# Attention and routed-expert layer on one core: the row maxima reach the score operand through TensorE and ScalarE instead of a transfer, with a new order of the work

## What is computed

```python
q, k, v = x @ wq + bq, x @ wk + bk, x @ wv + bv      # 16 heads of 8; rotary turn of q and k
scores = einsum('bhqd,bhkd->bhqk', q, k) / sqrt(8) + causal
x = layernorm(x + (softmax(scores) @ v) @ wo + bo)
idx = argmax(softmax(x.reshape(4096, 128) @ wg))     # 8 experts, first 512 tokens of each kept
x = layernorm(x + gate * (x @ W[idx].T + b[idx]))    # zero for tokens beyond an expert's 512
```

## Time and profile before

| | |
|---|---|
| median of 3 runs | 418.27 us (418.15 to 418.33) |
| the profiled execution | 417.29 us, span 415.5 us |
| busy in the span | TensorE 340.7, VectorE 326.3, ScalarE 269.9, GpSimd 285.5 us |
| DMA | 48.76 MB, 150727 packets; hardware queue of SyncE 58.9% of 16 engines' span, of ScalarE 3.0% |

### The profile page before, as it was taken

One profiled execution on the slowest core, in us unless ns is written; L12 is line 12 of the kernel. 1 busy time (PEld: TensorE's weight loads), 2 busy tenths in 40 slices (PEclk: granted clock), 3 DMA queues, 4 the chain that ended last, 5 costly groups with the idle time before them and its releaser, 6 DMA issues.

```text
span 415.5 us, 11631 instructions
## 1 busy us (share of the span) xinstructions
PE 340.7 (82%) x4230; PEld 279.9 (67%) x4230; DVE 326.3 (79%) x871; ACT 269.9 (65%) x633; POOL 285.5 (69%) x508
## 2 busy tenths in 40 slices
PE   4445596989989988898899989998999896987781
PEld 4334384868777877787777868786878785866561
DVE  5678664768989997999898989998989985875454
ACT  5252385758677866868595859695968585778500
POOL 6273337376688877787778787888879785575543
PEclk9968587999999999999999999999999999999976
DMA  5297948686968586857767676768586869310000
GB/s 153 76 174 143 144 114 127 106 147 117 143 120 160 108 141 132 163 100 148 138 134 132 138 136 126 146 118 167 110 162 113 157 112 165 24 43 2 16 13 25
DMA packets 150727, 48.76 MB, mean 117 GB/s; under 512 B 113311, under 2 KB 146979, under 8 KB 150670
## 3 DMA queue, kind: packets, MB, share of 16 engines
q1 hardware_dynamic: 144766, 43.70, 58.9%
q10 hardware_dynamic: 5184, 2.36, 3.0%
q0 software_dynamic: 720, 1.97, 1.5%
HBM read 28.60 MB, written 14.68 MB: 104 GB/s over the span
## 4 chain that ended last, share of the span: by engine, by line
PE 39%; DVE 14%; DMA 13%; ACT 13%; SPq 8%; issue 7%; POOL 2%; ACTq 2%; DVEq 0%; POOLq 0%
DMA q_plain<-max_rows 7%; DMA q_diag<-plain_parts 6%; PE ps_m L1051 4%; PE ps_ab L1137 4%; PE ps_ab L1121 4%; PE ps_pv L1152 4%; ACT high L693 3%; PE ps_m L1053 3%; PE ps_m L1052 3%; PE ps_ab L1105 3%; ACT ps_ab L697 3%; SPq L445 3%; SPq L489 3%; DVE row_max L911 2%; DVE low L901 2%
## 5 line engine op out<-in xcount | busy, mean ns | idle before, releaser
L693 ACT ACTIVATE high<-ps_ab 128x448 f16<-128x448 f32 (+1 forms) x192 | 100.9, 525 | 41.6 <-PE ps_ab L1121 40.9
L911 DVE TENSOR_REDUCE row_max<-ps_ab 128x2 f32<-128x512 f32 (+3 forms) x176 | 109.5, 628 | 12.7 <-PE ps_ab L1137 12.4
L540 POOL TENSOR_TENSOR low<-probs,high 128x384 f16<-128x384 f32 (+1 forms) x64 | 64.4, 1016 | 13.0 <-ACT probs L697 11.7
L901 DVE TENSOR_TENSOR low<-ps_ab,high 128x448 f16<-128x448 f32 (+1 forms) x80 | 47.1, 589 | 28.3 <-ACT ps_ab L697 28.3
L697 ACT ACTIVATE ps_ab<-ps_ab 128x448 f32<-128x448 f32 (+1 forms) x128 | 67.7, 529 | 0.0
L1121 PE MATMUL ps_ab<-q_plain,k_diag 128*128 128x128 bf16 (+1 forms) x768 | 66.5, 214 | 0.0
L1137 PE MATMUL ps_ab<-k_plain,q_diag 128*128 128x192 bf16 (+3 forms) x512 | 66.1, 243 | 0.0
L1152 PE MATMUL ps_pv<-v_mov,high 128*128 128x64 bf16 x768 | 64.6, 194 | 0.9 <-ACT low L701 0.7
L1152 PE MATMUL ps_pv<-v_mov,low 128*128 128x64 bf16 x768 | 64.4, 193 | 0.0
L1099 PE MATMUL ps_ab<-mask_a_bf,ident_bf 128*128 128x128 bf16 (+2 forms) x176 | 45.3, 257 | 19.5 <-DMA q_diag<-plain_parts 12.6
L1105 PE MATMUL ps_ab<-mask_b_bf,ident_bf 128*128 128x128 bf16 (+1 forms) x192 | 47.5, 247 | 15.2 <-DMA q_plain<-max_rows 6.1
(11 more groups left out here) (188 smaller groups left out, 928.5 us busy)
## 6 DMA issues: line engine op xcount, KB each, us to landing
plain_parts<-rot SPq DMA_DIRECT2D x180, 64.0 KB, 2.2
k_plain<-plain_parts SPq DMA_DIRECT2D x16, 384.0 KB, 4.2
q_diag<-plain_parts SPq DMA_DIRECT2D x32, 192.0 KB, 5.6
q_plain<-plain_parts SPq DMA_DIRECT2D x16, 384.0 KB, 4.8
k_diag<-plain_parts SPq DMA_DIRECT2D x32, 192.0 KB, 4.2
v_mov<-v_parts SPq DMA_DIRECT2D x64, 48.0 KB, 2.0
x_in<-in_L_attn_x_dram SPq DMA_DIRECT2D x16, 128.0 KB, 5.4
out_dram<-y_out POOLq DMA_DIRECT2D x15, 128.0 KB, 2.5
```

Source lines behind the costliest of these rows:

```text
L540: pool.tensor_tensor(fine(low, k), kept_probs(k), fine(high, k), ALU.subtract).then_inc(s_["low_pool"], 1)
L693: act.activation(fine(high, k), b_scores(k), ACT.Exp, scale=SCALE)
L901: dve.tensor_tensor(fine(low, k), b_scores(k), fine(high, k), ALU.subtract)\
L911: last = dve.tensor_reduce(row_max[:, NBLK - 1 - j, groups[0]:groups[-1] + 1], scores[:, :, col:col + width(j)], AX.X, ALU.max)
```

## The change

- `max_parts` gets 96 zero columns at its front, then 24 columns for each row block and half of the heads. "ex" becomes eight matmuls of 64 columns, whose stationary operand is a window of 120 columns that ends with the 24 wanted, so that the parts come out in rows 96 to 119 of `ps_n`, 256 columns for each half of the heads.
- ScalarE copies rows 96 to 119 of `ps_n` straight into `q_plain`, 24 rows of 4 x 256 columns, twice. `max_rows`, its two DMAs and the semaphore of their landing go. The copies wait for `b_ready` of two sequences earlier, b0 for `maxrows_done`.
- `LOWS` goes from DPADPDADPDAP to DPADPDDPDDAP: chunk 6 goes from way A to D and chunks 8 and 9 swap P and D for D and D with chunk 7 now P. Six rests lie on VectorE (chunks 0, 3, 5, 6, 8, 9), four on GpSimd (1, 4, 7, 11), two on ScalarE (2, 10).
- SyncE's list in a step becomes: x_in; the six writes of rot_1; q_plain; first half of k_diag; the four writes of rot_2; the two of rot_3; second half of k_diag; k_plain and q_diag once the writes have landed; v_mov.
- All positions are new. Around the maxima TensorE's order becomes: loc, b11, pv7, pv8, pv9, sub10, **ex**, e0, e1, pv10, pv11, a0, **b0**, b1, a1, e2, a2, e3, a3, turn, b2, a4, b3, y. ScalarE keeps exp of b11, low10, **maxrows**, rot1, copy, exp of b0. VectorE: a10, last logits piece, low9, the last gate piece of the sequence before, kept, rope, add, inv, gate, statistics, gate, sel0, gate, inv, a0, a1, low0. GpSimd: low4, out, low7, parts, seen, low11, rot, norm, rest pieces, low1.

The diff, less the tables of positions that are not spoken of:

```diff
-LOWS = "DPADPDADPDAP"
+LOWS = "DPADPDDPDDAP"
 PE_AT = dict(
-    b=(162, 163, 167, 169, 177, 180, 183, 190, 197, 198, 203, 208),
+    b=(176, 178, 187, 189, 195, 198, 205, 211, 215, 217, 222, 227),
-    a=(91, 93, 97, 100, 104, 114, 118, 123, 124, 127, 132),
-    pv=(171, 186, 189, 192, 199, 206, 207, 213, 215, 216, 218, 220), ex=147, turn=230, y=234, x1t=249, logits=259,
-    loc=268, v=112, xt=1, qk=9, e=(274, 278, 288, 293))
+    a=(111, 115, 118, 120, 124, 132, 133, 137, 145, 150, 154),
+    pv=(199, 207, 210, 213, 220, 221, 225, 228, 230, 231, 236, 238), ex=169, turn=250, y=254, x1t=270, logits=276,
+    loc=290, v=129, xt=2, qk=27, e=(298, 299, 309, 311))
...
-        max_parts = sb("max_parts", [128, NBLK, 64], bf)
-        max_rows = sb("max_rows", [2 * MAX_ROWS, S], bf)
+        max_parts = sb("max_parts", [128, SCORE_ROWS + NBLK * 2 * MAX_ROWS], bf)
...
                     after(sp, "y_ready", n - KEPT + 1)
                     sp.dma_start(x_in[n % KEPT][:, :, :], of_seq(x_t, n)).then_inc(s_["x_loaded"], 16)
-                if b_ahead:
-                    after(sp, "b_ready", b - 2, NB, NB)
-                    load_q_plain(b, p)
...
                 if b_ahead:
+                    after(sp, "b_ready", b - 2, NB, NB)
+                    load_q_plain(b, p)
                     load_k_diag(b, p, 0)
                 write(rot_2, 1, "rot2_done")
+                write(rot_3, 2, "rot3_done")
                 if b_ahead:
                     load_k_diag(b, p, 1)
-                write(rot_3, 2, "rot3_done")
-                if has(b) and not is_step(s, 0):
-                    load_v(b, p)
                 if has(a):
                     after(sp, "parts_written", a, PARTS_WRITTEN, PARTS_WRITTEN)
...
-                if is_step(s, 0):
+                if has(b):
                     load_v(b, p)
...
                         after(act, "ex_ready", b, 1, 1)
-                        after(act, "maxrows_loaded", b, 2 * 16)
-                        for jj in range(2):
-                            last = act.activation(max_rows[:, :].rearrange("m (i jj r) -> m jj i r", i=2, jj=2)[:, jj],
-                                                  ps_n[64 * jj:64 * jj + 2 * MAX_ROWS, 0:2 * BLK]
-                                                  .rearrange("m (i r) -> m i r", i=2), ACT.Copy)
+                        after(act, "b_ready", b - 2, NB, NB)
+                        for half_at in range(2):
+                            last = act.activation(q_plain[pb_][SCORE_ROWS:ONE_ROW, 4 * half_at:4 * half_at + 4, :],
+                                                  ps_n[SCORE_ROWS:ONE_ROW, S * half_at:S * half_at + S].unsqueeze(1)
+                                                  .broadcast_to([MAX_ROWS, 4, S]), ACT.Copy)
                         last.then_inc(s_["maxrows_done"], 1)
-                        after(act, "maxrows_done", b, 1, 1)
-                        after(act, "pv_ready", b - 2, NB, NB)
-                        for half_at in range(2):
-                            act.dma_start(q_plain[pb_][SCORE_ROWS:SCORE_ROWS + MAX_ROWS, 4 * half_at:4 * half_at + 4, :],
-                                          max_rows[MAX_ROWS * half_at:MAX_ROWS * half_at + MAX_ROWS, :].unsqueeze(1)
-                                          .broadcast_to([MAX_ROWS, 4, S])).then_inc(s_["maxrows_loaded"], 16)
...
-                            after(pe, "maxrows_loaded", c, 2 * 16, 2 * 16)
+                            after(pe, "maxrows_done", c, 1, 1)
...
-                        for i in range(NBLK // 2):
-                            mm = pe.matmul(ps_n[:, BLK * i:BLK * i + BLK],
-                                           max_parts[:, 2 * i:2 * i + 2, :].rearrange("p i m -> p (i m)"), stacked_bf[:, :],
-                                           start=(i == 0), stop=True, skip_group_check=True)
+                        for half_at in range(2):
+                            for j in range(NBLK):
+                                at, to = MAX_ROWS * (2 * j + half_at), S * half_at + BLK * j
+                                mm = pe.matmul(ps_n[0:ONE_ROW, to:to + BLK], max_parts[:, at:at + ONE_ROW], stacked_bf[:, :],
+                                               start=(half_at == 0 and j == 0), stop=True, skip_group_check=True)
```

More of the change, by code:

```diff
@@ L64 @@
 N_FIRST = 4
-LOWS = "DPADPDADPDAP"
+LOWS = "DPADPDDPDDAP"
 SLOTS = 64
 PE_AT = dict(
-    b=(162, 163, 167, 169, 177, 180, 183, 190, 197, 198, 203, 208),
-    sub=(153, 172, 174, 175, 181, 184, 194, 200, 202, 205, 209, 212),
-    a=(91, 93, 97, 100, 104, 114, 118, 123, 124, 127, 132),
-    pv=(171, 186, 189, 192, 199, 206, 207, 213, 215, 216, 218, 220), ex=147, turn=230, y=234, x1t=249, logits=259,
-    loc=268, v=112, xt=1, qk=9, e=(274, 278, 288, 293))
+    b=(176, 178, 187, 189, 195, 198, 205, 211, 215, 217, 222, 227),
+    sub=(180, 191, 192, 202, 204, 208, 216, 223, 224, 229, 232, 237),
+    a=(111, 115, 118, 120, 124, 132, 133, 137, 145, 150, 154),
+    pv=(199, 207, 210, 213, 220, 221, 225, 228, 230, 231, 236, 238), ex=169, turn=250, y=254, x1t=270, logits=276,
+    loc=290, v=129, xt=2, qk=27, e=(298, 299, 309, 311))
@@ L74 @@
 ACT_AT = dict(
-    b=(151, 152, 154, 157, 192, 193, 194, 196, 202, 204, 205, 209),
-    low=(155, 156, 158, 159, 160, 198, 199, 200, 206, 207, 210, 212), copy=(201, 214), attn=217, x1h=259, xh=5,
-    v1=97, maxrows=147, rot1=21, egate=267, route=272)
+    b=(152, 153, 157, 158, 192, 193, 198, 199, 203, 205, 208, 210),
+    low=(155, 156, 159, 160, 196, 197, 200, 201, 204, 206, 211, 214), copy=(202, 215), attn=218, x1h=259, xh=2,
+    v1=97, maxrows=148, rot1=21, egate=271, route=273)
 DVE_AT = dict(
-    low=(160, 163, 165, 167, 172, 174, 177, 193, 195, 205, 206, 221),
@@ L80 @@
-    a=(89, 91, 94, 97, 100, 105, 109, 111, 128, 134, 140), sel=(280, 290), inv=(212, 218), add=339, z1=230,
-    x1=(234, 235), stats2=341, x1l=240, xl=5, vrest=104, lg=(258, 260, 263, 264, 265, 266), rope=16,
-    g=(271, 274, 278, 279, 284))
+    low=(163, 169, 171, 172, 192, 193, 197, 203, 205, 209, 213, 225),
+    a=(96, 98, 101, 103, 104, 110, 113, 130, 134, 137, 143), sel=(285, 294), inv=(217, 223), add=344, z1=234,
+    x1=(239, 240), stats2=347, x1l=259, xl=4, vrest=109, lg=(263, 264, 266, 268, 270, 272), rope=22,
@@ L83 @@
+    g=(276, 282, 284, 286, 338))
 POOL_AT = dict(
-    low=(129, 135, 136, 139, 141, 143, 145, 146, 148, 149, 150, 192), norm=(195, 196), rs1=202, parts=80, vparts=76,
-    seen=211, rot=2, rest=(5, 6, 9), out=334)
-LAST_AT = [dict(e=(286, 287, 301, 307), sel=(287, 331), add=337), dict()]
+    low=(128, 134, 136, 137, 140, 142, 143, 144, 147, 148, 149, 150), norm=(194, 195), rs1=202, parts=81, vparts=75,
+    seen=210, rot=1, rest=(4, 5, 7), out=333)
+LAST_AT = [dict(e=(305, 313, 328, 331), sel=(292, 339), add=343), dict(g=(276, 282, 284, 286, 319))]
@@ L262, in layer_kernel @@
         names += """w_loaded vw_loaded ident_loaded late_loaded tables_loaded x_loaded parts_written
-                    aops_loaded0 aops_loaded1 bops_loaded0 bops_loaded1 maxrows_loaded v_loaded
+                    aops_loaded0 aops_loaded1 bops_loaded0 bops_loaded1  v_loaded
                     one_loaded stored""".split()
@@ L320, in max_part @@
         def max_part(i):
-            return max_parts[:, :, 0:2 * MAX_ROWS].rearrange("p j (half t m) -> p j half t m", half=2, t=3)[:, :, :, i, :]
+            return max_parts[:, SCORE_ROWS:].rearrange("p (j half t m) -> p j half t m", j=NBLK, half=2, t=3)[:, :, :, i, :]
         def by_half(t):
@@ L542, in _ @@
             pool.memset(minus_half[:, :], -0.5)
-            pool.memset(max_parts[:, :, :], 0.0)
+            pool.memset(max_parts[:, :], 0.0)
             pool.memset(words(q_diag[0][:, :, :, :, :].rearrange("p g j h r -> p (g j h r)")), 0.0)
```

## The result

The changed kernel takes 405.18 us (median of 4, 404.66 to 406.61) against 418.21 us, a ratio of 0.970 (95% interval 0.967 to 0.972): faster by 3.0%. The forecast was 404.4 in a range of 396 to 414. The total was right within 0.8 us; where the 13 us came from was not.

The account below looks back on a forecast made before the run. No engine full; waits between engines, in the maxima's and q_diag's loops, set the 21.7 us period. Gains of 8.4 steady, 4.0 start and 1.5 tail total 13.9: 417.29 to 403.4 profiled, 404.4 with the median's 0.98 offset; range 396 to 414.

Parts of the forecast that it names:

- The steady period: Time per repeat in the steady part: forecast to fall from 21.7 to 21.0 us, gaining 0.7 x 12 = 8.4 us.
- the other moves: Position changes other than putting e0 behind ex: priced at zero, with the range meant to hold them.
- VectorE's floor: VectorE's busy time per period, called the hard floor: 19.1 us before, 19.7 with one more subtraction of 0.62 us.
- rival 1: VectorE's gated sums stop waiting for GpSimd, freeing 1.3 us a period: period 20.4, about 397 us; chance 0.10.
- SyncE's loop: Loop from ex through rot_1's writes and SyncE's issues to q_diag's landing and a0: period at least 20.6 us after the change.
- rival 2: v_mov's new place fills SyncE's queue, so each a0 waits for q_diag: 23.2 us per period, 431 us; chance 0.09.
- Maxima without a transfer: Around ex: matmuls and two ScalarE copies of 1.04 us replace the transfer; first exp 2.3 us earlier relative to ex.
- this ring: Path from ex through the maxima to b0 and the first exp: priced as a floor of 20.0 us per period.
- The q_diag loop: Before the change, ex through rot_1's writes and SyncE's issues to q_diag's landing and a0: computed at 22.0 us per period.
- SyncE's list: SyncE's reordered issues, first write to end of q_diag's issue: 14.6 instead of 15.3 us, including a new 1.6 us landing wait.
- The sixth rest: One more VectorE subtraction of 448 columns per period, 0.62 us; with one input in PSUM, it slows nothing beside GpSimd.
- Start: First periods: first rest at 46.9 instead of 49.54 us, gaining 2.6, plus 0.7 in each of two periods: 4.0 us.

Follow-up runs that it names:

- e0: Not a run: a piece of TensorE's work, which the change puts right behind ex; the text gives no run of this name and no measured time.
- e1: The changed kernel with VectorE's `below` and `rank` moved right after `top`, ahead of the tenth reduction of pass a: 391.8 us, 0.937 of the kernel before.
- e3: The kernel before with only the maxima placed by TensorE and ScalarE; old order, LOWS and SyncE list: 7.2 us gained by the medians.
- e7: The changed kernel with the maxima again copied to max_rows and sent by two DMAs: median 418.92 us, 1.011 of the kernel before.
- e4: The kernel before with only SyncE's new list, maxima still sent by transfer: 0.975 of the kernel before, steady period 20.95 us.
- e10: The changed kernel with GpSimd's output moved after `seen`, ahead of chunk 11's rest instead of chunk 7's: 426.5 us.
- e8: The changed kernel with `below` made in its old place by two scalar-form instructions instead of one with two SBUF tensors: ten of 24 took 1.79 us.

## Why the prediction was right, and where its steps were wrong

**The total, and its three terms.** Steady 8.4, start 4.0, tail 1.5 us were forecast; measured are 1.9, 7.6 (9.14 less the 1.57 of a later first ex) and 2.8. The steady part gave 6.5 us less than forecast, start and tail 4.9 more, and the errors cancel. That the total came within 0.8 us was luck.

**The steady period: wrong.** The step that failed is "the other moves cannot be priced one by one; I put them at zero". VectorE's floor was not 19.7 but 252.57 / 260 x 21.82 = 21.2 us: nearly all of the 1.5 more are the waits behind GpSimd that the new positions brought, 1.7 by their means. The move that did it is in GpSimd's list: the rest of chunk 7 went directly behind the output's issue. I had this wait as rival 1, with the opposite sign: I saw it in the gated sum, asked whether it would end, and did not ask what else reads SBUF next to GpSimd's new list. The rival gave 1.3 us back; the truth was 1.7 taken. (Its P of 20.4 also lay below the 20.6 that I had just given SyncE's loop as a floor.) Without the held `below` (e1) the period is 20.35, below my 21.0 and near the 20.6 of SyncE's loop. What holds it there was not tried: from 80 to 340 us TensorE waits for q_diag three times, 2.2 us in all, and VectorE is busy for 95%.

**The signs.** No engine waits for q_diag ahead of a0 from 80 to 340 us, as forecast. v_mov's issues take 4.2 and 4.3 us in the two periods that I read, above the 4 us that I had named for rival 2, but without its q_diag waits, as x_in's fell to 0.54. The gated sum, rival 1's sign, rose to 1.17. The maxima are 21.8 us apart and not 21.0: that sign failed.

**VectorE above 92% busy: right, for the wrong reason.** It is 97%, because a held instruction counts as busy.

**Maxima without a transfer: right in size, wrong in place.** The copies take 1.01 us (forecast 1.04):

```profile
L723 ACT ACTIVATE q_plain<-ps_n x32: 1001/1008/1020, 40.9 to 362.2; 24x1024 bf16<-24x1024 f32 x32
```

ex takes 0.58 instead of 0.4; b0 comes 3.35 us after ex (236.05 - 232.70; forecast 3.4), the exp 3.99 after it (forecast 3.7). But in the old order this ring was not the bound (e3: 21.68). My "21.7 - 2.3 + 0.6" took it for one, on the word of the chain, which shows the transfer in most periods. The q_diag loop, computed at 22.0, was longer, and the prediction had that number. In the new order, where b0 stands close behind ex, the transfer does cost: about 0.04 of the time before (e7).

**SyncE's list: right, undersized.** Forecast 0.7 us less from first write to q_diag's issue; 1.9 measured (e4), since six writes run on without a gap for k_diag (4.45 against 3.67 + 1.50 + a gap) and v_mov's 2.59 is out. The landing wait was forecast at 1.6 and is 1.0 (226.43 - 225.41). Rival 2 saw v_mov's swelling (4.92; 5.42 was the guess), and its answer, that only one of the two pays, holds.

**The sixth rest: right.** VectorE's rests of 448 columns take 0.617 us, before 0.621: one input in PSUM, and GpSimd doesn't slow them, which no row had shown.

**Start: right in mechanism, undersized.** The first rest starts at 47.95 (forecast 46.9), not 49.54:

```profile
46.75 1.29 DVE L900 TENSOR_REDUCE row_max<-ps_ab 128x2 f32<-128x512 f32 x2
47.95 0.55 DVE L890 TENSOR_TENSOR low<-ps_ab,high 128x384 f16<-128x384 f32 x1
```

The rest of the 9.1 us is the list and the rows in the second and third period, where I had allowed 0.7 each: e4 alone gives 3.8 in the first three, e3 2.9, together 5.9, and the positions 3.3 more.

**Tail.** b0 comes 2.84 us after the last ex (363.39 - 360.55), not 3.9; the forecast was 2.5.

## What to carry to other kernels

When two engines hold each other back, the price of moving a piece depends on what the other engine runs at that moment, and on what stands ready behind it: `below` was free inside GpSimd's issue when the next piece came 0.9 us or more after it, and took 1.6 us more when a rest stood directly behind. Look for small instructions whose mean exceeds their minimum by far: a busy share near 100% can be waits, and one move of two 16-column instructions was worth 3.3% here. Of two near-critical loops, compute both before pricing a gain: the chain shows the one that ended last, which may be slack the moment the other is touched. And put behind a queue's heavy loads what nobody waits for, because the backlog is paid by the next one in line.

## What the runs showed of the hardware that I had not expected

- A VectorE instruction of 16 fp32 columns with two tensors from SBUF, started 0.15 us or more into GpSimd's issue of a DMA (0.81 us), is held to the end of the GpSimd rest that stands ready behind the issue, 1.77 us instead of 0.165, in 8 of 12 cases. The issue alone doesn't do it: in the kernel before 13 of 13 that started 0.13 to 0.59 us into it took at most 0.174 us, where no GpSimd instruction followed for 0.86 us or more. Nor are those held that start with the issue, to 0.01 us (`rank` in e1, the gated sum in e10). Why the hold begins before the rest is shown to start is open.
- The scalar form with one SBUF tensor and a scalar per partition is held too (1.79 us in 10 of 24, e8); a reciprocal and a reduction with one SBUF tensor weren't (e10).
- SyncE's issue of four 48 KB loads takes 2.6 us behind two writes of 64 KB (before), or 4.9 directly behind three loads of 192 to 384 KB (e4), and the next issue fell from 3.70 to 0.54 us in exchange.
- Loading 120 stationary columns took longer than 128: 0.129 to 0.135 us against 0.095 to 0.102 in the ex of before, and ex's eight matmuls took 0.58 us, 0.18 more than I had read from pv's.
